# Expert routing with scan instructions and per-tile transposes, and the last layer norm in eight buffers in place, in a one-layer decoder kernel

## What is computed

```python
def _layernorm(x, axis=-1, eps=1e-05):
    m = jnp.mean(x, axis=axis, keepdims=True)
    v = jnp.var(x, axis=axis, keepdims=True)
    return (x - m) / jnp.sqrt(v + eps)
...
    xf = x.reshape(-1, D)
    scores = xf @ router_w.T
    top_v, top_i = jax.lax.top_k(scores, TOP_K)
    routing_w = jax.nn.softmax(top_v, axis=-1)
    out = jnp.zeros_like(xf)
    for e in range(NUM_EXPERTS):
        w_e = jnp.sum(jnp.where(top_i == e, routing_w, 0.0), axis=-1)
        h = jax.nn.gelu(xf @ expert_w1[e].T, approximate=False)
        out = out + h @ expert_w2[e].T * w_e[:, None]
```

## Time and profile before

| | us |
|---|---|
| median of 3 runs | 1164.17 (1163.9 to 1164.26) |
| the profiled run | 1166.83 |
| its span, first to last instruction | 1164.9 |

### The profile page before, as it was taken

One profiled execution on the slowest core, in us unless ns is written; L12 is line 12 of the kernel. 1 busy time (PEld: TensorE's weight loads), 2 busy tenths in 40 slices (PEclk: granted clock), 3 DMA queues, 4 the chain that ended last, 5 costly groups with the idle time before them and its releaser, 6 DMA issues.

```text
span 1164.9 us, 24917 instructions
## 1 busy us (share of the span) xinstructions
PE 948.5 (81%) x8069; PEld 762.1 (65%) x8070; DVE 813.1 (70%) x1196; ACT 481.8 (41%) x1132; POOL 712.0 (61%) x461
## 2 busy tenths in 40 slices
PE   7984079998999989768878249999999999999940
PEld 4542079897888888746656237777777777777730
DVE  4899999999999998248888764444444444444435
ACT  3676334444555554436656223223333223333315
POOL 3576499999999999300000055666666667666522
PEclk9998589999999999979999569999999999999985
DMA  3262102221121212477674412222222222222236
GB/s 103 64 129 35 45 19 69 68 68 57 56 68 68 67 46 67 164 261 270 203 249 163 168 29 38 44 43 45 45 45 41 45 45 43 44 44 43 30 91 220
DMA packets 69916, 100.24 MB, mean 86 GB/s; under 512 B 9248, under 2 KB 51680, under 8 KB 68928
## 3 DMA queue, kind: packets, MB, share of 16 engines
q1 hardware_dynamic: 52816, 76.85, 21.1%
q0 software_dynamic: 15904, 18.66, 10.1%
q10 hardware_dynamic: 1152, 4.19, 0.9%
HBM read 73.82 MB, written 26.25 MB: 86 GB/s over the span
## 4 chain that ended last, share of the span: by engine, by line
PE 45%; issue 17%; POOL 17%; DVE 11%; DMA 5%; ACT 4%; SPq 0%; POOLq 0%; DVEq 0%; ACTq 0%
PE psum L760 16%; PE psum L768 10%; POOL mid L1191 9%; PE psum L770 5%; PE psum L619 3%; DMA sum_dram<-arena,mid 2%; PE psum L599 2%; PE psum L662 2%; POOL arena L1196 2%; POOL arena L1182 1%; PE psum L752 1%; POOL arena L1202 1%; DVE arena L1579 1%; PE psum L688 1%; PE psum L602 1%
## 5 line engine op out<-in xcount | busy, mean ns | idle before, releaser
L619 PE MATMUL psum<-consts,mid 128*128 128x128 f32 x2176 | 252.8, 278 | 52.1 <-POOL mid L1191 52.1
L760 PE MATMUL psum<-arena 128*128 128x128 f16 x3408 | 286.5, 220 | 4.1 <-issue 2.6
L760 PEld LDWEIGHTS psum<-arena 128*128 x3408 | 239.2, 98 | 75.3 <-issue 9.6
L619 PEld LDWEIGHTS psum<-consts,mid 128*128 128x128 f32 x2176 | 247.9, 193 | 61.8 <-issue 48.4
L1191 POOL TENSOR_TENSOR mid<-arena 128x2304 f32<-128x2304 f32 (+1 forms) x62 | 251.3, 4075 | 9.6 <-POOL arena L1182 7.6
L768 PE MATMUL psum<-arena 128*128 x568 | 215.1, 380 | 4.9 <-DVE arena L1736 1.2
L1269 POOL DMA_INDIRECT sum_dram<-arena,mid x71 | 141.4, 1991 | 43.4 <-issue 20.5
L1745 DVE SCALAR_TENSOR_TENSOR arena<-psum,arena 128x256 f32<-128x256 f32 x71 | 34.4, 484 | 186.2 <-ACT arena L1088 120.1
L1430 DVE TENSOR_REDUCE arena<-mid 128x272 f32<-128x4624 f32 x32 | 158.9, 4967 | 1.7 <-ACT mid L894 1.2
L1088 ACT ACTIVATE arena<-psum,arena 128x256 f32<-128x256 f32 x71 | 33.7, 475 | 296.4 <-PE psum L770 296.4
L770 PE MATMUL psum<-arena 128*128 x568 | 154.8, 273 | 0.0
(11 more groups left out here) (196 smaller groups left out, 1443.8 us busy)
## 6 DMA issues: line engine op xcount, KB each, us to landing
arena<-w_t SPq DMA_DIRECT2D x64, 256.0 KB, 2.8
arena<-w_t SPq DMA_DIRECT2D x16, 1024.0 KB, 10.5
arena<-x SPq DMA_DIRECT2D x32, 128.0 KB, 2.1
arena<-x_dram SPq DMA_DIRECT2D x8, 512.0 KB, 5.0
arena<-ctx_t SPq DMA_DIRECT2D x8, 512.0 KB, 5.8
arena<-ctx SPq DMA_DIRECT2D x8, 512.0 KB, 6.5
x_dram<-mid SPq DMA_DIRECT2D x8, 512.0 KB, 3.3
arena<-sum_dram SPq DMA_DIRECT2D x8, 512.0 KB, 5.0
```

The source lines that it names most:

```text
L619: last = nc.tensor.matmul(psum[:, u, c * P:(c + 1) * P], products[half][:, w, c * P:(c + 1) * P], ident, start=(a + w == 0 and c == 0), st ...
L760: last = nc.tensor.matmul(dst, block_of(w, e, 0, c * F + j * P, P), x[:, u, c * P:(c + 1) * P], start=(k == 0 and c == 0), stop=(k == 2 an ...
```

## The change

- **The last norm 2.** For sequence 7, PE transposes tile by tile, each as soon as its norm is done, into four banks. ACT copies tile by tile, and the router's products wait for each tile's copy. The low part of expert 6 that stood before this norm moves behind it. The low parts of expert 7 are spread out: one half before the logits' copy, one while PE makes the counts, and two behind `routed`. PE waits for the last of them before its first lot. On ACT the high parts and the copy of x2 stand behind the tile copies.
- **Routing.** Counts are laid out expert by expert, and one scan instruction over 256 elements gives the running sums over all tiles and experts. The sum of the experts before is subtracted later, on eight numbers. Another scan over 8 numbers gives the lots. The constant of the triangle is lowered by one, so that one sum replaces two. Places are reduced straight to integers, which the marks compare without a conversion. The source rows are made first, and POOL's row fetch waits for them alone (`sources_made`). The rest of POOL's work waits for `routed`.
- **The last norm.** Eight buffers of four tiles lie where the expert weights were. All eight loads are issued at once. The statistics are combined by DVE's aggregate instruction, tile by tile. ACT norms three of a group's four tiles in place, POOL the fourth, and the store goes out of the same buffer.

The diff, cut to its core:

```diff
@@ -78,11 +78,10 @@
...
-        i < j,
+        (i < j) - 1.0,
...
@@ -262,11 +259,11 @@
...
-        sum3 = next_low("end", 4, QT, E)
-        out_rows = next_low("end", 2, QT, E)
...
+        sum3 = carve(big, 0, GROUPS3, QT, E)
+        stats3 = next_low("end", GROUPS3, QT, 6)
+        norm3_of = next_low("end", GROUPS3, QT, 2)
+        mean3, rstd3 = norm3_of[:, :, :, 0], norm3_of[:, :, :, 1]
+        bias3 = next_low("end", GROUPS3, QT)
...
@@ -573,15 +568,10 @@
...
-            def load_sums(g, v):
-                if g >= 4:
-                    sp.wait_ge(out_ready, QT * (g - 3))
-                sp.dma_start(sum3[:, v], sum_group[g].rearrange("(p t) e -> p t e", p=P)).then_inc(y_loaded[v], 16)
             sp.wait_ge(y_added, 16 * LOTS)
-            for g in range(TILES // QT):
-                load_sums(g, g % 4)
-            for u in (0, 1):
-                sp.wait_ge(out_stored[u], 16 * (TILES // QT // 2))
+            for g in range(GROUPS3):
+                sp.dma_start(sum3[:, g], sum_group[g].rearrange("(p t) e -> p t e", p=P)).then_inc(y_loaded[g], 16)
+            sp.wait_ge(out_stored, 16 * GROUPS3)
...
@@ -719,15 +709,24 @@
...
             pe.wait_ge(sum2_done, T // P)
-            transpose_x2(B - 1, 1)
-            route(B - 1)
-
-
-            pe.wait_ge(picked_made, 1)
+            for t in range(QT):
+                pe.wait_ge(normed2, QT * (B - 1) + t + 1)
+                for c in range(C):
+                    last = nc.tensor.transpose(psum[:, t, c * P:(c + 1) * P], x1_n[:, 1, t, c * P:(c + 1) * P], ident)
+                last.then_inc(tile_turned, 1)
+            for t in range(QT):
+                pe.wait_ge(tile_copied, t + 1)
+                for c in range(C):
+                    last = nc.tensor.matmul(psum[:, 7, t * N_EXP:(t + 1) * N_EXP], x2_t[:, c, t * P:(t + 1) * P],
+                                            router_w[:, c, :], start=(c == 0), stop=(c == C - 1))
+            last.then_inc(router_done, 1)
+
+
+            pe.wait_ge(gap_and_picks, 2)
...
@@ -1059,15 +1058,19 @@
...
-            high_parts(N_EXP - 1, 0)
+            for t in range(QT):
+                act.wait_ge(tile_turned, t + 1)
+                nc.scalar.activation(x2_t[:, :, t * P:(t + 1) * P], psum[:, t, 0:C * P].rearrange("p (c n) -> p c n", n=P),
+                                     ACT.Copy).then_inc(tile_copied, 1)
+            high_part(N_EXP - 1, 0, 0)
             keep_x2(B - 1, 1)
-            x2_transposed(B - 1)
+            high_part(N_EXP - 1, 0, 1)
+
+
+            nc.scalar.activation(count_psum, consts[:, AT_COUNT:AT_COUNT + P], ACT.Copy).then_inc(count_and_gap, 1)
...
@@ -1110,18 +1113,16 @@
...
-            def norm3(g, u, v):
-                if g >= 2:
-                    act.wait_ge(out_stored[u], 16 * (g // 2))
+            def norm3(g):
                 act.wait_ge(shift3_made, g + 1)
-                for t in range(QT):
-                    nc.scalar.activation(out_rows[:, u, t, :], sum3[:, v, t, :], ACT.Identity, bias=mean3[:, v, t:t + 1],
-                                         scale=rstd3[:, v, t:t + 1]).then_inc(out_ready, 1)
-                act.wait_ge(out_ready, QT * (g + 1))
-                act.dma_start(out_group[g].rearrange("(p t) e -> p t e", p=P),
-                              out_rows[:, u]).then_inc(out_stored[u], 16)
-            for g in range(TILES // QT):
-                norm3(g, g % 2, g % 4)
+                for t in range(QT - 1):
+                    nc.scalar.activation(sum3[:, g, t, :], sum3[:, g, t, :], ACT.Identity, bias=bias3[:, g, t:t + 1],
+                                         scale=rstd3[:, g, t:t + 1]).then_inc(out_ready, 1)
+                act.wait_ge(out_ready, (QT - 1) * (g + 1))
+                act.wait_ge(last_ready, g + 1)
+                act.dma_start(out_group[g].rearrange("(p t) e -> p t e", p=P), sum3[:, g]).then_inc(out_stored, 16)
...
@@ -1243,7 +1244,7 @@
...
                                         .to_broadcast([P, PART, SLOTS]), ALU.mult).then_inc(slot_tiles, 1)
-            pool.wait_ge(routed, 1)
...
@@ -1258,6 +1259,7 @@
...
                     pool.wait_ge(f_tables_stored, 48)
...
@@ -1275,25 +1277,18 @@
...
                     fetch_gates(s - 4, s % 4)
-            for g in range(TILES // QT):
-                root(rstd3[:, g % 4, :], QT, B + g + 1)
+            for g in range(GROUPS3):
+                root(rstd3[:, g, :], QT, B + g + 1)
+                pool.wait_ge(rstd_ready, B + g + 1)
+                t = QT - 1
+                nc.gpsimd.tensor_scalar(sum3[:, g, t, :], sum3[:, g, t, :], mean3[:, g, t:t + 1], rstd3[:, g, t:t + 1],
...
@@ -1561,8 +1556,9 @@
...
-                if past(b, 1):
-                    low_part(b - 1, 1, 1)
+                if more:
+                    if past(b, 1):
+                        low_part(b - 1, 1, 1)
...
@@ -1606,33 +1602,31 @@
...
             norm2(B - 1, 1)
-            for k in range(2):
-                for half in range(2):
-                    low_part(N_EXP - 1, k, half)
...
+            low_part(N_EXP - 1, 0, 0)
             copy_logits(B - 1, 1)
...
-            nc.vector.tensor_tensor(top_v[:, 1, :], top_v[:, 1, :], top_v[:, 0, :], ALU.subtract).then_inc(gap_made, 1)
+            nc.vector.tensor_tensor(top_v[:, 1, :], top_v[:, 1, :], top_v[:, 0, :], ALU.subtract).then_inc(gap_and_picks, 1)
...
-            nc.vector.tensor_tensor(picked, chosen[:, 0], chosen[:, 1], ALU.add).then_inc(picked_made, 1)
-            dve.wait_ge(counted, 1)
-            tile_count = psum[:, 1, 0:TILES * N_EXP].rearrange("p (t n) -> p t n", n=N_EXP)
-
-            n_scan = 1
-            done(nc.vector.tensor_copy(upto[0], tile_count), scan_step, n_scan)
-            at, hop = 0, 1
-            while hop < TILES:
-                nc.vector.tensor_copy(upto[1 - at][:, 0:hop, :], upto[at][:, 0:hop, :])
-                n_scan += 1
-                done(nc.vector.tensor_tensor(upto[1 - at][:, hop:, :], upto[at][:, hop:, :], upto[at][:, 0:TILES - hop, :],
-                                             ALU.add), scan_step, n_scan)
-                at, hop = 1 - at, 2 * hop
+            nc.vector.tensor_tensor(picked, chosen[:, 0].rearrange("p t n -> p n t"), chosen[:, 1].rearrange("p t n -> p n t"),
+                                    ALU.add).then_inc(gap_and_picks, 1)
+            nc.vector.memset(ends[:, 0:1], 0.0).then_inc(scan_step, 1)
+            low_part(N_EXP - 1, 0, 1)
+            dve.wait_ge(routing_products, 1)
+            flat = "p a b -> p (a b)"
+            done(nc.vector.tensor_tensor_scan(upto.rearrange(flat), psum[:, 1, 0:TILES * N_EXP], picked.rearrange(flat), 0.0,
+                                              ALU.add, ALU.max), scan_step, 2)
+            nc.vector.tensor_copy(ends[:, 1:], upto[:, :, TILES - 1]).then_inc(scan_step, 1)
+            nc.vector.tensor_tensor(place.rearrange(flat), upto.rearrange(flat), psum[:, 0, 0:TILES * N_EXP],
+                                    ALU.add).then_inc(place_made, 1)
+            dve.wait_ge(scan_step, 3)
 
             n_lots = 0
...
@@ -1640,41 +1634,32 @@
...
-            lots_done(nc.vector.tensor_scalar(lots_i, upto[at][:, TILES - 1, :], float(P - 1), None, ALU.add))
+            lots_done(nc.vector.scalar_tensor_tensor(lots_i, ends[:, 1:], float(P - 1), ends[:, 0:N_EXP], ALU.add, ALU.subtract))
             lots_done(nc.vector.tensor_scalar(lots_i, lots_i, P.bit_length() - 1, None, ALU.logical_shift_right))
             lots_done(nc.vector.tensor_copy(lots_n, lots_i))
-            lots_done(nc.vector.tensor_copy(lots[:, 0, :], lots_n))
-            now, hop = 0, 1
-            while hop < N_EXP:
-                nc.vector.tensor_copy(lots[:, 1 - now, 0:hop], lots[:, now, 0:hop])
-                lots_done(nc.vector.tensor_tensor(lots[:, 1 - now, hop:], lots[:, now, hop:], lots[:, now, 0:N_EXP - hop], ALU.add))
-                now, hop = 1 - now, 2 * hop
-            lots_end = lots[:, now, :]
-
-            done(nc.vector.tensor_tensor(place, upto[at], tile_count, ALU.subtract), place_made, 1)
-            done(nc.vector.tensor_tensor(place, place, psum[:, 0, 0:TILES * N_EXP].rearrange("p (t n) -> p t n", n=N_EXP),
-                                         ALU.add), place_made, 2)
+            lots_done(nc.vector.tensor_tensor_scan(lots_end, lots_n, lots_n, 0.0, ALU.add, ALU.max))
+
             lots_done(nc.vector.tensor_tensor(lots_n, lots_end, lots_n, ALU.subtract))
-            lots_done(nc.vector.tensor_scalar(lots_n, lots_n, float(P), None, ALU.mult))
-            done(nc.vector.tensor_tensor(place, place, lots_n.unsqueeze(1).to_broadcast([P, TILES, N_EXP]), ALU.add), place_made, 3)
-            done(nc.vector.tensor_tensor(placed, chosen, place.unsqueeze(1).to_broadcast([P, TOP, TILES, N_EXP]), ALU.mult),
-                 spot_step, 2)
-            done(nc.vector.tensor_reduce(spot, placed, op=ALU.add, axis=AX.X), spot_step, 3)
-            done(nc.vector.tensor_copy(spot_i[:, 0], spot), spot_step, 4)
```

(53 more changed lines are left out.)

89 lines of the change are left out of this document (39 added, 50 removed).

## The result

| | before | after |
|---|---|---|
| median | 1164.04 us (1162.39 to 1164.26, 4 runs) | 1153.38 us (1152.73 to 1154.71, 4 runs) |
| profiled run | 1166.83 us, span 1164.9 | 1154.71 us, span 1151.6 |

A forecast was written before the change was run, and what follows sets the result against it. PE's expert loop bounds the kernel, untouched; gains lie before and behind it. 3.1 + 4.2 - 0.5 + 8.5 = 15.3 us less takes the median of 1164.17 to 1148.9, own range 1147.5 to 1150.5, wider range 1146.0 to 1153.0.

The forecast's parts named there:

- Part A: Last norm 2 and its transposes, from POOL's power to the logits copy: 7.15 against 10.22 us, 3.1 us less.
- The clock bound: Last norm 2: were the granted clock still high, transposes and router products would take about half, 2.5 us less.
- Part B: The routing's scan stretch up to the row marks: 8.84 us before, 4.6 after, 4.2 us less (3.5 to 4.5).
- Part C: Fetch of the first rows, up to PE's start: 5.12 us before, 5.6 after, 0.5 more (0.4 less to 2.0 more).
- a held fetch: POOL's first row fetch held over one of DVE's low halves, so PE starts at 5.6 us: 0.5 us more.
- Part D: The last norm, first load to end of span: 35.5 us before, 27.0 after, 8.5 us less (5.5 to 9.0).
- so 1.8 and hidden: Last norm, POOL per group: power 1.01 plus one tile row, nearest row 0.735, up to 0.9, hidden under DVE's 2.10.
- it takes 3.4 to the end as before: Program's end: from the last store's issue at 23.1 us to the end of the span, 3.4 us, giving 26.5.
- mixed transfers: Last norm: half a microsecond added for loads and stores that mix, taking 26.5 to 27.0 us.
- rival 2: Last norm: transfers bind at 290 GB/s, 29 us, end at 31, 4 us more than forecast: 1152.9 us; chance 0.14.

## Why the prediction was right and wrong

- **Direction: right, and the mechanism but for the program's end.** Both chains were where the chain of waits put them, and the loop handed their gain on whole, at the same period.
- **Part A: 3.1 forecast, 3.4 measured.** The power took 1.0, and PE set the pace. The router's products began 0.2 us before the transposes had ended and took 3.42, not 3.58. The clock bound, 2.5 us, was far: where the granted clock fell later than the first transposes, up to 0.65 us more was won.
- **Part B: 4.2 forecast, 3.9 measured.** The scan is what I took, 0.69. The strided product cost 0.34 us more than its dense like, which I had priced at nothing and bounded at 0.5, and the picks, ahead of this stretch and with strided reads too, took 0.62 instead of 0.43. The Trainium skill, "DVE: opcode table, instruction layouts, handler registers and perf-mode slots", Datapath and trigger behaviour, says that the built-in scan runs at half throughput; by it, the run agrees: 0.69 us for 256 elements, as a plain operation took for 512.
- **Part C: 0.5 more forecast, nothing measured.** POOL's fetch, which began 0.19 us before the low halves, was not held. PE was late by its own wait, end of the halves plus 1.0 us for the word and what follows it, where I had 0.6; with that wait moved it started 3.08 us behind the fetch. Together the routing stood at 6.8 in the sum; in the pairs of runs it gave 6.9 us, and 7.0 to 7.3 by the stretches. From the power to PE's first transpose the profile has 40.4 us where it had 47.5, so 7.1 less: the 0.5 us charged for a held fetch and the 0.3 us more won in part A outweighed the 0.5 us that the strided reads cost.
- **Part D: 8.5 forecast, 3.8 measured: this is the step that failed.** Its first part held: the first store at 8.4 forecast and 8.45 measured, no waits for stores, DVE's own pace 2.04 where I had 2.10, and the aggregates 0.53 us a group cheaper than the seven steps. Two terms were wrong. First, POOL's tile was priced from a row of another operation, 0.735 us, at most 0.9, "so 1.8 and hidden". It takes 1.23, which makes POOL the bound at 2.33 a group; the last store was issued at 24.75 instead of 23.1, **1.65 us**. Second, "it takes 3.4 to the end as before" carried on a number without asking what it was made of. In the kernel before two paths ended within 0.3 us of each other, the last store's and POOL's DRAIN, and the DRAIN was the later one. The change shortened the one and, by giving POOL a tile more in each group, kept the other near: the end came 6.67 us behind the last store's issue, in both profiles of the changed kernel. Had the store set it, the end would have come near 1148, by SP's last step at 1147.77; **3.6 us**. The store's own last leg took 3.0 us and not the 3.9 that I had put there (3.4 and 0.5 for mixed transfers), so 1.65 + 3.6 - 0.9 makes the 4.4 by which 31.4 lies over 27.0. In the run with POOL out of the last two groups the stage took 26.75 us, and the sum had said 27.0, but this is partly luck: POOL's tile still set the pace of six groups there, the last store was issued at 23.4 instead of 23.1, its way to the end took 3.4 us instead of 3.9, and DRAIN and store ended together.
- **The base.** The sum was made against one profiled execution, 2.7 us above the median, and then taken off the median. The last norm took 34.9 us in another execution, not 35.5, so 0.6 of the forecast's 8.5 was never to be had. One profile is a loose base: the two spans of before are 1164.9 and 1161.4, and PE's way to the first send alone scattered by 1.6 us over all profiles.
- **Range.** Its upper end, 1153.0, left out the far half of rival 2, and nothing in it stood for an end set by something else than the last store. Rival 2 gave 1152.9, nearly the measured time, by a mechanism that did not happen: in the run with POOL out of two groups all bytes were through in 26.75 us. Its price was also too low by its own rows: a load's landing and the last store's end hold about 2 us each beyond the transfer (3.27 and 3.4, less 1.3), so 29 us of transfer would have ended near 33 and not 31.

## What to carry to other kernels

When a change shortens a tail, list every engine's last instruction and what comes behind it at the program's end, not only the engine that ends last now: a second path that ends within 0.3 us of the first takes over at once. Work that is handed to an idle engine must be priced by a row of the same operation in the same form; where none exists, carry the price at which that engine becomes the bound as a rival with a time of its own. Judge an edit of 1 us by its stretch between two fixed instructions, since medians of four runs here part only about 2 us.
